# Attention stage with projections: explicit step lists over two images per loop body, and an fp32 product for the last key block

## The chip, the cores and the metric

The kernel runs on one core of a Trainium2 chip. The metric is the device time of one execution in microseconds. A core has five engines with their own instruction queues, each strictly in order: PE (TensorE, matrix products into PSUM), DVE (VectorE), ACT (ScalarE), POOL (GpSimd) and SP (SyncE, which here only issues DMAs). They meet through semaphores: an instruction adds to one when it ends, and another engine's queue waits until a count is reached.

## What is computed

The reference is a chain of six blocks on 32 images of 32 x 32 tokens with 64 channels. The change lies in one of them, attention with projections:

```python
q = jnp.einsum('bnf,of->bno', x, Wq) + bq
k = jnp.einsum('bnf,of->bno', x, Wk) + bk
v = jnp.einsum('bnf,of->bno', x, Wv) + bv
scores = jnp.einsum('bnf,bmf->bnm', q, k) / TEMP      # 1024 x 1024 an image
alpha = jax.nn.softmax(scores, axis=-1)
out = jnp.einsum('bnm,bmf->bnf', alpha, v)
...
t = t + _L3_attn_ref(_ln_t(t), ...)                   # _ln_t: normalise over 64 channels
```

## The kernel before

After a setup the kernel runs five stages, one after the other with a barrier between: the two convolution-like blocks, attention without projections (`stage_attend`, here the second stage), the expert pooling, attention with projections (`stage_attend_qkv`, the fourth stage, 1806 to 2575 us), and the routed experts. All tokens stay in one SBUF tensor, `tokens`.

**Numbers as pairs.** fp32 accuracy is kept with fp16 matmuls by splitting a number into a high and a low fp16 part. Weighing probabilities with values takes three products per key block: high x high, high x low, low x high (L1921, L1923, L1925).

**An image in the fourth stage.** It has 8 query tiles of 128 tokens (NT = 8). Ahead of the tiles come the normalisation (helpers L68 to L138: sum and centring on DVE, square on ACT, sum of squares on DVE, inverse root and scaling on POOL, the high part on ACT, the low part on POOL, eight transposes on PE, a copy on DVE) and five projections through one PSUM bank `ps_w`, each PE, then ACT (high part), then DVE (low part, L1739, L1742, L1745): two halves of q, two halves of k, one v. Then for each tile g:
- range: two matmuls into `ps_a` (L1889), which exists once; DVE takes the negated row maximum (L1767), and SP copies it as a row into `qm` with a small DMA (L1720). Four semaphores `max_rowed` tell when a row has landed.
- score: sixteen matmuls of 128 columns into one of two buffers `ps_s` (L1905, L1907).
- ACT takes the exponential into `pr` (fp32, a ring of RING = 4) at L1823, and its fp16 high part `prh` at L1827; POOL subtracts for the low part `prl` (L1850).
- weigh: 24 matmuls of 65 columns into one of two places of `ps_o` (L1921 to L1925); the 65th column sums the probabilities.
- for every two tiles, DVE takes the reciprocal (L1774) and adds the divided result to `tokens` (L1777, two steps of 64 columns).

**What sets the order.** Each engine's queue is written by `stream` (L1049): for each tile m of an image, `near` (projections of the next image, step m), `step` (range of tile m + 3, score of tile m, weighing of tile m - 3, as far as the engine has a part in it) and `far` (normalisation of the image after that, step m). All engines use the same frame; one image after the next, two images in one loop body. Waits of note: the exponential of tile g waits until POOL's low part of tile g - 4 is done and the high part until tile g - 4 is weighed (L1822, L1826); weighing an even tile waits until the two before it have been added (L1914).

```python
at = tile_at(i, h, m + LEAD)          # PE, step: range of a later tile
at = tile_at(i, h, m) if m >= 0 else None   # score of this one
at = tile_at(i, h, m - LAG)           # weighing of an earlier one
```

Of the kernel before, what the change touches and what calls it, by code (L numbers as in the profile page):

```python
# [6 lines left out]
ALU = mybir.AluOpType  # L7
# [5 lines left out]
P = 128  # L13
# [1639 lines left out]
def stage_attend_qkv(net, d):  # L1653
# [4 lines left out]
    RING, LAG, LEAD = 4, 3, 3  # L1658
    with ExitStack() as ctx:
# [23 lines left out]
        tv = net.t[:].rearrange("p (i h) g c -> p i h g c", h=2)  # L1683
# [7 lines left out]
        def count(at, lag=0):  # L1691

            i, h, m = at
            return NT * (2 * i + h) + m - lag + 1

        def pair_count(at, lag=0):

            i, h, m = at
            return (NT // 2) * (2 * i + h) + (m - lag) // 2 + 1

        def row_count(at, lag=0):

            i, h, m = at
            return 16 * ((NT // RING) * (2 * i + h) + (m - lag) // RING + 1)

        def past(at, lag):

            return tile_at(at[0], at[1], at[2] - lag) is not None

        with nc.Block() as block:  # L1710
            @block.sync
            def _(sp):

                def copy_and_turn(n, h):
                    for k in range(2):
                        sp.wait_ge(proj_high, piece_count(n, PROJ, k))
                        sp.dma_start(qm[h][0:C, half_of(k)], qx[h][0:C, half_of(k)]).then_inc(copied, 16)
                    for g in range(NT):
                        sp.wait_ge(maxed, piece_count(n, NT, g))
                        sp.dma_start(qm[h][C:C + 1, P * g:P * g + P], nmax[:, g:g + 1]).then_inc(max_rowed[g % RING], 16)  # L1720

                sp.wait_ge(set_up, 1)
                with sp.Fori(0, PAIRS) as i:
                    for h in range(2):
                        copy_and_turn(2 * i + h, h)
                sp.wait_ge(copied, 32 * B)
                for r in range(RING):
                    sp.wait_ge(max_rowed[r], 16 * (NT // RING) * B)

            @block.vector  # L1730
            def _(dve):
                def near(i, h, m):
                    n, k = 2 * i + h, m - 1
                    if not 0 <= k < PROJ:
                        return
# [13 lines left out]
                def far(i, h, m):  # L1749
                    n1, w = base + 2 * i + h + 1, wk[h]  # L1750
                    if m == 0:
                        norm_sum(nc, ln, n1, tv[:, i, h], w)
                    if m == 1:
                        norm_centre(nc, ln, n1, tv[:, i, h], w)
                    if m == 2:
                        norm_sumsq(nc, ln, n1, w)
                    if m == 7:
                        take_turned(nc, ln, n1, w, ps_w[:].bitcast(F16))

                def step(i, h, m):  # L1760
                    at = tile_at(i, h, m + LEAD)
                    if at:
                        g = at[2]
                        dve.wait_ge(ranged, count(at))
                        if past(at, NT):
                            dve.wait_ge(max_rowed[g % RING], row_count(at, NT))
                        nc.vector.tensor_reduce(nmax[:, g:g + 1], ps_a[:], AX.X, ALU.max,  # L1767
                                                negate=True).then_inc(maxed, 1)
                    at = tile_at(i, h, m - LAG)
                    if at and at[2] % 2:  # L1770

                        ia, ha, g = at
                        dve.wait_ge(weighed, count(at))
                        nc.vector.reciprocal(rinv[:], outs[:, :, C]).then_inc(inverted, 1)  # L1774
                        dve.wait_ge(inverted, pair_count(at))
                        for k in range(2):
                            ins = nc.vector.scalar_tensor_tensor(tv[:, ia, ha, g - 1 + k], outs[:, k, 0:C],  # L1777
                                                                 rinv[:, k:k + 1], tv[:, ia, ha, g - 1 + k],
                                                                 ALU.mult, ALU.add)
                        ins.then_inc(added, 1)  # L1780

                for h in range(2):
                    set_ones(nc, wk[h])
                    nc.vector.memset(vh[h][:, :, C:C + 1], 1.0)
                    nc.vector.memset(vl[h][:, :, C:C + 1], 0.0)
# [6 lines left out]
                stream(dve, step, near, far, LAG, near_first=True, lead=LEAD)  # L1792
# [3 lines left out]
            def _(act):  # L1796
                def near(i, h, k):
                    if k >= PROJ:
                        return
# [547 lines left out]
```

## Time and profile before

| | |
|---|---|
| median of 3 runs | 2982.1 us (2976.99 to 2982.51) |
| the profiled execution | 2982.43 us, span 2980.6 us |
| PE | busy 2303.2 us, 77% of the span |
| DVE | 2260.9 us, 76% |
| ACT | 2107.7 us, 71% |
| POOL | 1694.9 us, 57% |
| mean granted TensorE clock | 0.921 |
| fourth stage, steady part | about 1866 to 2550 us, clock 1.00 |

The shares are means over stages with different limits. The change touches the fourth stage alone, so it is read in windows of that stage. A busy PE includes the time in which matmuls overlap in the pipeline; for what PE can take, the distance from one start to the next is read. A row of the timeline gives start, length, engine, line and operation, and in brackets the idle time before with what ended it.

### The profile page before, as it was taken

The numbers are of one execution on the slowest core, as the hardware profiler recorded it, in microseconds if no ns is written. First come the engines' busy times: TensorE is split into PE (matmuls) and PEld (weight loads), VectorE is DVE, ScalarE is ACT, GpSimd is POOL, SyncE is SP. The second block draws the span as 40 slices with busy tenths as digits, with TensorE's granted clock in tenths as the row PEclk, the third lists the DMA queues.
The fourth block names the chain that finished last, engine by engine and source line by source line (L and its number), as shares of the span: only waits on it lengthen the run. The fifth ranks groups of instructions, "written<-read, shape, count | busy, mean of one in ns | idle before, by whom it ended". The sixth has DMA issues, their size and how long they took to land. (4 is left out here: it accounts for less than half of the span.)

```text
span 2980.6 us, 85198 instructions
## 1 busy us (share of the span) xinstructions
PE 2303.2 (77%) x32988; PEld 1694.0 (57%) x32988; DVE 2260.9 (76%) x3654; ACT 2107.7 (71%) x3520; POOL 1694.9 (57%) x1370
## 2 busy tenths in 40 slices
PE   3777777787874999999645485888888888777777
PEld 1555555555552676777434473776777677544454
DVE  4677787777774899898766325888888888688887
ACT  2677777777773899999622112888888888677776
POOL 3577777777765222222266202998999899733331
PEclk9999999999996999999856566999999999799999
DMA  3211111111100000000000200000000000001001
GB/s 72 50 44 37 37 39 42 42 36 30 29 22 1 19 18 18 18 18 18 9 0 0 58 0 4 7 5 5 7 5 5 5 7 6 4 22 24 21 21 25
DMA packets 144660, 62.06 MB, mean 21 GB/s; under 512 B 118677, under 2 KB 127799, under 8 KB 144567
## 3 DMA queue, kind: packets, MB, share of 16 engines
q1 hardware_dynamic: 139565, 58.00, 9.1%
q10 hardware_dynamic: 4393, 2.77, 0.4%
q8 instruction: 64, 1.05, 0.1%
q14 instruction: 30, 0.24, 0.0%
q0 software_dynamic: 608, 0.01, 0.0%
HBM read 14.50 MB, written 8.39 MB: 8 GB/s over the span
## 5 line engine op out<-in xcount | busy, mean ns | idle before, releaser
L1850 POOL TENSOR_TENSOR a_prl<-a_pr,a_prh 128x1024 f16<-128x1024 f32 x256 | 544.3, 2139 | 38.1 <-ACT a_prh L1827 36.3
L1767 DVE TENSOR_REDUCE a_nmax<-a_ps_a 128x1 f16<-128x1024 f32 x256 | 312.1, 1219 | 29.3 <-PE a_ps_a L1889 27.3
L1198 DVE TENSOR_TENSOR a_exl<-a_ex,a_exh 128x1024 f16<-128x1024 f32 x224 | 275.6, 1260 | 29.6 <-ACT a_exh L1238 28.5
L1827 ACT ACTIVATE a_prh<-a_pr 128x1024 f16<-128x1024 f32 x256 | 270.6, 1057 | 8.2
L1823 ACT ACTIVATE a_pr<-a_ps_s 128x1024 f32<-128x1024 f32 x256 | 259.4, 1013 | 0.0
L1905 PE MATMUL a_ps_s<-a_qx,a_kh 128*128 128x128 f16 x2048 | 257.9, 220 | 0.3 <-DMA a_qm<-a_nmax 0.3
L1907 PE MATMUL a_ps_s<-a_qm,a_kl 128*128 128x128 f16 x2048 | 257.9, 220 | 0.0
L1233 ACT ACTIVATE a_ex<-a_ps_s,a_shift 128x1024 f32<-128x1024 f32 x224 | 242.9, 1099 | 0.5 <-PE a_ps_s L1281 0.5
L2152 ACT ACTIVATE f_mixed_s<-f_ps_e,f_gates 128x64 f32<-128x64 f32 x1024 | 212.8, 425 | 41.8 <-PE f_ps_e L397 37.0
L1921 PE MATMUL a_ps_o<-a_vh,a_prh 128*128 128x65 f16 x2048 | 216.8, 196 | 3.4 <-POOL a_prl L1850 3.4
L1905 PEld LDWEIGHTS a_ps_s<-a_qx,a_kh 128*128 128x128 f16 x2048 | 200.6, 98 | 31.0 <-issue 1.0
L1907 PEld LDWEIGHTS a_ps_s<-a_qm,a_kl 128*128 128x128 f16 x2048 | 201.1, 98 | 29.9 <-issue 0.6
L114 POOL TENSOR_TENSOR a_w_hl<-a_xn,a_w_hl 128x512 f16<-128x512 f32 x32 | 36.0, 1124 | 318.4 <-ACT a_w_hl L106 318.4
L1923 PE MATMUL a_ps_o<-a_vl,a_prh 128*128 128x65 f16 x2048 | 217.0, 193 | 0.0
L1925 PE MATMUL a_ps_o<-a_vh,a_prl 128*128 128x65 f16 x2048 | 216.1, 193 | 0.0
L1280 PE MATMUL a_ps_s<-a_w_xT 128*128 128x512 f16 x512 | 196.5, 384 | 22.1 <-ACT a_ex L1233 13.0
L1889 PE MATMUL a_ps_a<-a_kh,a_qx 128*128 128x512 f16 x512 | 156.0, 387 | 64.5 <-DVE a_nmax L1767 64.4
L1281 PE MATMUL a_ps_s<-a_w_xT,a_xTb 128*128 128x512 f16 x512 | 195.0, 381 | 0.0
L90 POOL TENSOR_TENSOR f_w_var<-f_w_ss,eps 128x8 f32<-128x8 f32 x64 | 12.8, 200 | 320.1 <-DVE f_w_ss L85 320.1
L1921 PEld LDWEIGHTS a_ps_o<-a_vh,a_prh 128*128 128x128 f16 x2048 | 191.8, 97 | 4.0 <-POOL a_prl L1850 2.6
L1925 PEld LDWEIGHTS a_ps_o<-a_vh,a_prl 128*128 128x128 f16 x2048 | 192.1, 97 | 0.0
L1923 PEld LDWEIGHTS a_ps_o<-a_vl,a_prh 128*128 128x128 f16 x2048 | 191.6, 99 | 0.0
(351 smaller groups left out, 8535.7 us busy)
## 6 DMA issues: line engine op xcount, KB each, us to landing
tokens<-in_x_dram SPq DMA_DIRECT2D x32, 256.0 KB, 2.9
bl_qg<-bl_qk_high SPq DMA_DIRECT2D x128, 64.0 KB, 2.0
bl_km<-bl_qk_high SPq DMA_DIRECT2D x256, 32.0 KB, 2.0
a_xTb<-a_w_xT SPq DMA_DIRECT2D x64, 128.0 KB
out_dram<-tokens SPq DMA_DIRECT2D x32, 256.0 KB, 2.6
bl_qg<-bl_qk_low SPq DMA_DIRECT2D x64, 64.0 KB, 2.0
bl_km<-bl_qk_low SPq DMA_DIRECT2D x128, 32.0 KB, 2.0
a_qm<-a_qx SPq DMA_DIRECT2D x64, 64.0 KB, 2.0
```

The costliest lines, as they stand in the source:

```text
L1198: nc.vector.tensor_tensor(exl[:, at[2]], exps(at), exh[:, at[2]], ALU.subtract).then_inc(low, 1)
L1233: nc.scalar.activation(exps(at), ps_s[:, m % 2], ACT.Exp, bias=shift[:]).then_inc(exped, 1)
L1767: nc.vector.tensor_reduce(nmax[:, g:g + 1], ps_a[:], AX.X, ALU.max, negate=True).then_inc(maxed, 1)
L1823: nc.scalar.activation(pr[:, r], ps_s[:, m % 2], ACT.Exp).then_inc(exped, 1)
L1827: nc.scalar.activation(prh[:, r], pr[:, r], ACT.Copy).then_inc(high, 1)
L1850: nc.gpsimd.tensor_tensor(prl[:, r], pr[:, r], prh[:, r], ALU.subtract).then_inc(low, 1)
L1905: nc.tensor.matmul(out, kh[ha][:, keys], qx[ha][:, queries], start=True, stop=False, skip_group_check=True)
L1907: last = nc.tensor.matmul(out, kl[ha][:, keys], qm[ha][:, queries], start=False, stop=True, skip_group_check=True)
L1921: nc.tensor.matmul(out, high_j, vh[ha][:, j], start=(j == 0), stop=False, skip_group_check=True)
L1923: nc.tensor.matmul(out, high_j, vl[ha][:, j], start=False, stop=False, skip_group_check=True)
L1925: last = nc.tensor.matmul(out, low_j, vh[ha][:, j], start=False, stop=(j == NT - 1), skip_group_check=True)
L2152: ins = nc.scalar.activation(mixed_s[:, h, e, g // 2], ps_e[:, g % BANKS, C * e:C * e + C], ACT.Identity, scale=gates[q][h][:, g, e:e + 1])
```

## The change

`stream` is left for this stage. Each engine gets a written list of steps for one body (one image), and `run_pairs` (L440) lays two bodies into the loop. AHEAD says which image a step belongs to: norm two images ahead, proj, copy, range_next and row_next one ahead, weigh_last and final_last one behind, the others the body's own. The order within a body differs from engine to engine and is no longer one frame by tiles. Among the differences: the exponential now waits for both the low part and the weighing of tile g - 4, and other steps may stand between it and the high part; DVE runs the norm steps 0 and 1 in front of the range step of tile 3; SP issues rows, then the copies, then the rows of the next image; ACT waits before a projection's high part until the image before last is through with the buffer.

```python
def iteration(i, k):                  # run_pairs, L445
    for stream, step in steps:
        n = i + ahead[stream]
        if not isinstance(i, int) or 0 <= n < B:
            streams[stream](n, step, (k + ahead[stream]) % 2)
```

The second part: of 8 key blocks, the last (SPLIT = 7) is weighed as one fp32 matmul from `pr` and a new fp32 tensor `vf`, in front of the others. So the high and the low parts of a tile are 896 columns instead of 1024, DVE gets one more instruction per image (`vf`, 64 columns) and its step for `vl` is 448 columns instead of 512.

```diff
-    RING, LAG, LEAD = 4, 3, 3
+    RING = 4
+    SPLIT = NT - 1
...
+        vf = [sb(f"vf{h}", [P, NT - SPLIT, C + 1], F32) for h in range(2)]
         pr = sb("pr", [P, RING, TOK], F32)
-        prh, prl = (sb(s, [P, RING, TOK], F16) for s in ("prh", "prl"))
+        prh, prl = (sb(s, [P, RING, P * SPLIT], F16) for s in ("prh", "prl"))
...
+        PE_STEPS = [("range", 3), ("proj", 0), ("score", 0), ("score", 1), ("range", 4), ("weigh_last", 5),
+                    ("proj", 1), ("score", 2), ("range", 5), ("weigh_last", 6), ("proj", 2), ("weigh_last", 7),
+                    ("score", 3), ("range", 6), ("weigh", 0), ("score", 4), ("range", 7), ("proj", 3), ("score", 5),
+                    ("weigh", 1), ("range_next", 0), ("proj", 4), ("score", 6), ("range_next", 1), ("weigh", 2),
+                    ("weigh", 3), ("range_next", 2), ("score", 7), ("norm", 5), ("weigh", 4)]
+        DVE_STEPS = [("norm", 0), ("norm", 1), ("range", 3), ("proj", 0), ("norm", 2), ("range", 4),
+                     ("final_last", 2), ("proj", 1), ("range", 5), ("final_last", 3), ("range", 6), ("proj", 2),
+                     ("range", 7), ("proj", 3), ("final", 0), ("range_next", 0), ("range_next", 1), ("proj", 4),
+                     ("final", 1), ("range_next", 2), ("norm", 5)]
+        ACT_STEPS = [("proj", 0), ("norm", 1), ("score", 0), ("proj", 1), ("cut", 0), ("score", 1), ("score", 2),
+                     ("proj", 2), ("cut", 1), ("cut", 2), ("score", 3), ("proj", 3), ("cut", 3), ("score", 4),
+                     ("norm", 4), ("cut", 4), ("score", 5), ("proj", 4), ("cut", 5), ("score", 6), ("score", 7),
+                     ("cut", 6), ("cut", 7)]
+        POOL_STEPS = [("norm", 2), ("cut", 0), ("norm", 3), ("cut", 1), ("cut", 2), ("cut", 3), ("norm", 4),
+                      ("cut", 4), ("cut", 5), ("cut", 6), ("cut", 7)]
+        SP_STEPS = [("row", 3), ("row", 4), ("row", 5), ("row", 6), ("row", 7), ("copy", 0), ("copy", 1),
+                    ("row_next", 0), ("row_next", 1), ("row_next", 2)]
+        AHEAD = {"norm": 2, "proj": 1, "copy": 1,
+                 "range_next": 1, "row_next": 1, "range": 0, "row": 0, "score": 0, "cut": 0, "weigh": 0, "final": 0, "weigh_last": -1, "final_last": -1}
+
+        def run(engine, steps, streams):
+
+            run_pairs(engine, steps, AHEAD, {s: streams[s.removesuffix("_next").removesuffix("_last")] for s, _ in steps})
...
+                def copy(n, k, h):
+                    sp.wait_ge(proj_high, piece_count(n, PROJ, k))
+                    sp.dma_start(qm[h][0:C, half_of(k)], qx[h][0:C, half_of(k)]).then_inc(copied, 16)
+
+                def row(n, g, h):
+                    sp.wait_ge(maxed, count(n, g))
+                    sp.dma_start(qm[h][C:C + 1, P * g:P * g + P], nmax[:, g:g + 1]).then_inc(max_rowed[g % RING], 16)
...
-                        ins = nc.vector.scalar_tensor_tensor(vl[h][:, :, 0:C], tiles(ps_w[:]), IWS,
-                                                             vh[h][:, :, 0:C], ALU.mult, ALU.subtract)
+                        nc.vector.tensor_scalar(vf[h][:, :, 0:C], tiles(ps_w[:])[:, SPLIT:NT], IWS, None, ALU.mult)
+                        ins = nc.vector.scalar_tensor_tensor(vl[h][:, 0:SPLIT, 0:C], tiles(ps_w[:])[:, 0:SPLIT], IWS,
+                                                             vh[h][:, 0:SPLIT, 0:C], ALU.mult, ALU.subtract)
...
+                def take_max(n, g, h):
+                    dve.wait_ge(ranged, count(n, g))
+                    if past(n, g, NT):
+                        dve.wait_ge(max_rowed[g % RING], row_count(n, g, NT))
+                    nc.vector.tensor_reduce(nmax[:, g:g + 1], ps_a[:], AX.X, ALU.max, negate=True).then_inc(maxed, 1)
...
+                    if not isinstance(n, int) or n >= 2:
+                        act.wait_ge(scored if k < 4 else weighed, NT * (n - 1))
...
+                def score(n, g, h):
+                    act.wait_ge(scored, count(n, g))
+                    if past(n, g, RING):
+                        act.wait_ge(low, count(n, g, RING))
+                        act.wait_ge(weighed, count(n, g, RING))
+                    nc.scalar.activation(pr[:, g % RING], ps_s[:, g % 2], ACT.Exp).then_inc(exped, 1)
+
+                def cut(n, g, h):
+                    act.wait_ge(exped, count(n, g))
+                    nc.scalar.activation(prh[:, g % RING], pr[:, g % RING, 0:P * SPLIT], ACT.Copy).then_inc(high, 1)
...
+                def cut(n, g, h):
+                    r = g % RING
+                    pool.wait_ge(high, count(n, g))
+                    nc.gpsimd.tensor_tensor(prl[:, r], pr[:, r, 0:P * SPLIT], prh[:, r], ALU.subtract).then_inc(low, 1)
...
+                def weigh(n, g, h):
+                    if g % 2 == 0 and past(n, g, 1):
+                        pe.wait_ge(added, pair_count(n, g // 2, 1))
+                    if g == 0:
+                        pe.wait_ge(proj_low, piece_count(n, PROJ, PROJ - 1))
+                    pe.wait_ge(low, count(n, g))
+                    out = outs[:, g % 2]
+                    for j in range(SPLIT, NT):
+                        nc.tensor.matmul(out, pr[:, g % RING, P * j:P * j + P], vf[h][:, j - SPLIT], start=(j == SPLIT),
+                                         stop=False, skip_group_check=True)
+                    for j in range(SPLIT):
+                        high_j, low_j = (s[:, g % RING, P * j:P * j + P] for s in (prh, prl))
+                        nc.tensor.matmul(out, high_j, vh[h][:, j], start=False, stop=False, skip_group_check=True)
+                        nc.tensor.matmul(out, high_j, vl[h][:, j], start=False, stop=False, skip_group_check=True)
+                        last = nc.tensor.matmul(out, low_j, vh[h][:, j], start=False, stop=(j == SPLIT - 1),
+                                                skip_group_check=True)
+                    last.then_inc(weighed, 1)
```

## Rows read from the trace of the kernel before

**Rows 1.** Windows view: stretch, length, busy us and count by engine, clock, DMA.
```profile
1865.51:2514.41 648.90, 566.92 (x10412) 457.89 (x10408) 549.96 (x821) 563.32 (x652) 589.77 (x340) 1.00 0.05 6
```

**Rows 2.** Source view of L74: count, min/median/max ns, first and last start.
```profile
L74 DVE SCALAR_TENSOR_TENSOR a_w_xc<-a_w_sum,tokens x29: 2364/2392/2505, 1872.1 to 2514.6; 128x512 f32<-128x512 f32 x29
```

**Rows 3.** Waits view, 1860 to 2550 us: us in total, times, longest.
```profile
PE a_ps_a L1889 <- DVE a_nmax L1767: 59.1, 119, 0.7
...
POOL a_w_var L90 <- DVE a_w_ss L85: 39.8, 29, 1.4
```

**Rows 4.** Timeline of DVE in two images: start us, length us, engine, line.
```profile
2150.64 1.23 DVE L1767 TENSOR_REDUCE a_nmax<-a_ps_a 128x1 f16<-128x1024 f32 x1
2151.78 0.16 DVE L1774 RECIPROCAL a_rinv<-a_ps_o 128x2 f32<-128x2 f32 x1
2152.09 0.47 DVE L1777 SCALAR_TENSOR_TENSOR tokens<-a_ps_o,a_rinv,tokens 128x64 f32 x2 [0.15 <-DVE a_rinv L1774]
2152.48 0.68 DVE L85 TENSOR_REDUCE a_w_ss<-a_w_sq 128x8 f32<-128x512 f32 x1
...
2153.67 1.21 DVE L1767 TENSOR_REDUCE a_nmax<-a_ps_a 128x1 f16<-128x1024 f32 x1
...
2164.98 0.69 DVE L138 COPY a_w_xT<-a_ps_w 128x1024 f16<-128x1024 f16 x1 [0.59 <-PE a_ps_w L128]
...
2167.75 0.68 DVE L69 TENSOR_REDUCE a_w_sum<-tokens 128x8 f32 x1
...
2170.44 2.39 DVE L74 SCALAR_TENSOR_TENSOR a_w_xc<-a_w_sum,tokens 128x512 f32<-128x512 f32 x1
```

**Rows 5.** Timeline of POOL beside that L74.
```profile
2170.15 2.13 POOL L1850 TENSOR_TENSOR a_prl<-a_pr,a_prh 128x1024 f16<-128x1024 f32 x1 [0.22 <-ACT a_prh L1827]
```

**Rows 6.** Timeline of ACT: a P part, C, E, C.
```profile
2154.63 0.60 ACT L1804 ACTIVATE a_kh<-a_ps_w 128x512 f16<-128x512 f32 x1 [0.73 <-PE a_ps_w L417]
...
2169.02 1.06 ACT L1827 ACTIVATE a_prh<-a_pr 128x1024 f16<-128x1024 f32 x1
...
2170.47 1.02 ACT L1823 ACTIVATE a_pr<-a_ps_s 128x1024 f32<-128x1024 f32 x1
2171.51 1.06 ACT L1827 ACTIVATE a_prh<-a_pr 128x1024 f16<-128x1024 f32 x1
```

**Rows 7.** Timeline of ACT, second stage: an exponential right behind another.
```profile
1202.46 1.10 ACT L1233 ACTIVATE a_whole<-a_ps_s,a_shift 128x1024 f32<-128x1024 f32 x1
1203.46 1.10 ACT L1233 ACTIVATE a_ex<-a_ps_s,a_shift 128x1024 f32<-128x1024 f32 x1
```

**Rows 8.** Timeline of PE: starts of P, R, S, W, P4 and R.
```profile
2154.22 0.38 PE L417 MATMUL a_ps_w<-a_w_xT,wb 128*128 128x512 f16 x1
2154.94 0.61 PE L1889 MATMUL a_ps_a<-a_kh,a_qx 128*128 128x512 f16 x2 [0.34 <-DVE a_nmax L1767]
2155.38 0.22 PE L1905 MATMUL a_ps_s<-a_qx,a_kh 128*128 128x128 f16 x1
...
2156.27 0.19 PE L1921 MATMUL a_ps_o<-a_vh,a_prh 128*128 128x65 f16 x1
...
2157.01 0.19 PE L409 MATMUL a_ps_w<-wa,a_w_xT 128*128 128x64 f16 x1
...
2157.48 0.60 PE L1889 MATMUL a_ps_a<-a_kh,a_qx 128*128 128x512 f16 x2
```

**Rows 9.** Timeline, first stage: DVE started ahead of POOL.
```profile
113.55 0.69 DVE L74 SCALAR_TENSOR_TENSOR bl_norm_xc<-bl_norm_sum,tokens 128x512 f32<-128x512 f32 x1
...
113.67 1.59 POOL L114 TENSOR_TENSOR bl_gate_hl<-bl_x,bl_gate_hl 128x512 f16<-128x512 f32 x1 [0.79 <-ACT bl_gate_hl L106]
```

**Rows 10.** Timeline of PE, second stage: fp32 matmuls, two records each.
```profile
1207.67 1.67 PE L1292 MATMUL a_ps_o<-a_xn,a_whole 128*128 128x65 f32 x14
...
1210.48 0.33 PE L1292 MATMUL a_ps_o<-a_xn,a_whole 128*128 128x65 f32 x2
1210.65 0.19 PE L1310 MATMUL a_ps_o<-a_w_hl,a_exh 128*128 128x65 f16 x1
```

More of the change, by code:

```diff
@@ L1756, in far @@
                         norm_sumsq(nc, ln, n1, w)
-                    if m == 7:
+                    if step == 5:
                         take_turned(nc, ln, n1, w, ps_w[:].bitcast(F16))
[L1760 to L1780, printed above, removed]
@@ new lines, in take_max, with final @@
+                def take_max(n, g, h):
[3 more added lines that the diff above has]
+                    nc.vector.tensor_reduce(nmax[:, g:g + 1], ps_a[:], AX.X, ALU.max, negate=True).then_inc(maxed, 1)
+                def final(n, p, h):
+                    dve.wait_ge(weighed, count(n, 2 * p + 1))
+                    nc.vector.reciprocal(rinv[:], outs[:, :, C]).then_inc(inverted, 1)
+                    dve.wait_ge(inverted, pair_count(n, p))
+                    for k in range(2):
+                        ins = nc.vector.scalar_tensor_tensor(net.t[:, n, 2 * p + k], outs[:, k, 0:C], rinv[:, k:k + 1],
+                                                             net.t[:, n, 2 * p + k], ALU.mult, ALU.add)
+                    ins.then_inc(added, 1)
@@ L1791, in _ @@
                 ins.then_inc(set_up, 1)
-                stream(dve, step, near, far, LAG, near_first=True, lead=LEAD)
+                run(dve, DVE_STEPS, {"norm": norm, "proj": proj_low_part, "range": take_max, "final": final})
                 dve.wait_ge(added, B * NT // 2)
@@ new lines, in norm, with rank @@
+                def norm(n, step, h):
+                    if not isinstance(n, int) or n >= 1:
+                        pe.wait_ge(proj_low, PROJ * n)
+                    turn(nc, ln, base + n + 1, wk[h], ps_w[:].bitcast(F16), net.ident16[:])
+                def rank(n, g, h):
+                    if g == 0:
+                        pe.wait_ge(proj_low, piece_count(n, PROJ, PROJ - 2))
+                    if past(n, g, 1):
+                        pe.wait_ge(maxed, count(n, g, 1))
+                    for half in range(2):
+                        keys = slice(512 * half, 512 * half + 512)
+                        last = nc.tensor.matmul(ps_a[:, keys], qx[h][:, P * g:P * g + P], kh[h][:, keys], start=True,
+                                                stop=True)
+                    last.then_inc(ranged, 1)
@@ new lines, in score @@
+                def score(n, g, h):
+                    pe.wait_ge(max_rowed[g % RING], row_count(n, g))
+                    if g == 0:
+                        pe.wait_ge(copied, 32 * n + 32)
+                    if past(n, g, 2):
+                        pe.wait_ge(exped, count(n, g, 2))
+                    queries = slice(P * g, P * g + P)
+                    for j in range(NT):
+                        keys, out = slice(P * j, P * j + P), ps_s[:, g % 2, P * j:P * j + P]
+                        nc.tensor.matmul(out, kh[h][:, keys], qx[h][:, queries], start=True, stop=False,
+                                         skip_group_check=True)
+                        last = nc.tensor.matmul(out, kl[h][:, keys], qm[h][:, queries], start=False, stop=True,
+                                                skip_group_check=True)
+                    last.then_inc(scored, 1)
@@ L1929, in _ @@
                 pe.wait_ge(set_up, 1)
-                stream(pe, step, near, far, LAG, lead=LEAD)
+                run(pe, PE_STEPS, {"norm": norm, "proj": project, "range": rank, "score": score, "weigh": weigh})
 ROUTE_STEPS = [("mix0", 0), ("mix0", 1), ("mix0", 2), ("mix0", 3), ("mix0", 4), ("mix0", 5), ("mix0", 6), ("mix0", 7),
```

166 lines of the change are left out of this document (37 added, 129 removed).

## The prediction

> Short names, for one image of 8 query tiles: R is the range pass of a tile (L1889), M its maximum on VectorE (L1767), S its scores (L1905, L1907), E the exponential, C and L the high and low cut (L1827, L1850), W the weighing (L1921 to L1925), F the final step of two tiles (L1774, L1777), P0 to P4 the projections, T the transposes. A prime marks a tile of the image before, an n one of the image after.
>
> **What bounds the kernel now.** I read the windows view of the middle of the stage first. The granted clock is 1.00 there, so nothing below is a clock effect; POOL is busy 91% of the time, ACT 87%, PE 87%, DVE 85% [rows 1]. No engine is full, and four are nearly so. Next the period: the line that centres the normalisation (L74) starts once an image, from 1872.1 to 2514.6 in 29 starts, so an image takes 642.5 / 28 = **22.95 us** [rows 2]. POOL's busy time in that is 589.8 x 22.95 / 648.9 = 20.9 us; two microseconds are idle everywhere. Where they go the waits show: PE stands 59 us before R until the maximum of the tile before is taken, and POOL 40 us until VectorE's sum of squares has come [rows 3]. PE and DVE pass one buffer (ps_a) and one pair of outputs (ps_o) back and forth in a fixed order by tiles. The DVE timeline shows the worst link: L74 lasts 2.39 us where its fastest instances, in other stages, take 0.69 [rows 4, 9]. Beside it stands a POOL instruction L1850 that started 0.29 us earlier at 2170.15 and ended at 2172.28; L74 ended at 2172.83, 0.55 us later [rows 4, 5]. All 29 instances are 2.36 to 2.51 us long [rows 2]. So a DVE instruction with two SBUF inputs stands still while POOL has one, and this kernel pays it every image. The other order exists too: where L74 starts 0.12 us before a POOL subtraction, L74 takes 0.69 us and POOL 1.59 [rows 9].
>
> **Costs of the change, per image.**
> POOL: L1850 shrinks from 1024 to 896 columns, 2.135 x 7/8 = 1.87 us, eight times: minus 2.1 us. POOL comes down to 18.8 us and is no longer the fullest.
> ACT: C goes from 1.06 to about 0.95 us (1024 columns take 1.06, 512 take 0.60, so 0.9 ns a column) [rows 6]. In the old order E and C of a tile follow each other, with C waiting for E's end: starts 1.04 us apart [rows 6]. In the new order an E is often followed by something that is ready, and then starts are 1.00 us apart for a 1.10 us instruction [rows 7], an overlap of 0.10. I take 0.92 for an E that takes 1.02. ACT falls from 20 to some 18 us.
> DVE: an added tensor_scalar of 64 columns (vf), not in the trace of before. Starts lie about 0.09 us closer than the durations are long (M is 1.23 us, the next start comes after 1.14). A reciprocal of 2 columns, 0.17 us, so makes 0.08; two steps of 64 columns with a second input move the next start by 0.39, 0.20 each. Between these I take 0.14 for vf, in the middle, since its width is that of the one and its single input that of the other [rows 4]. The step for vl is 64 columns shorter, minus 0.07. So DVE does not change by more than 0.1 us, less what L74's wait becomes.
> SP: R rows, copies and rows of the next image go in one written order. Row issues were spread over the whole image and are so again; each M is issued at least 3 us before its S, and the copies stand behind row 7, 7 us before S0 of the next image. I cost that at nothing; were a row late, S would wait by that much.
> PE: from start to start, S is 0.89 us, W 0.74 (24 matmuls, 31 ns each), R 0.43, P the same two 512-column matmuls (0.44), P4 0.47, and T, half as many matmuls as S, 0.45 [rows 8]. That is 8 x (0.89 + 0.74 + 0.43) + 4 x 0.44 + 0.47 + 0.45 = 19.2 us. Of W, three matmuls go (93 ns) and one fp32 matmul of 128x65 comes. The trace has the same form in the second stage: one of them, two records, stands 0.17 us from its start to the next matmul's; of seven in a row each further one adds (1.67 - 0.33) / 6 = 0.22 [rows 10]. The 0.17 comes behind a 512-column matmul that covers its first weight load (0.11 us, half of 0.22). Behind W's own 31 ns matmuls 0.08 of that load is bare, behind S or T 0.05. So W is 0.82 five times, 0.87 twice and 0.90 once: PE becomes 19.98 us. Bounds: 0.17 everywhere gives 19.8, 0.25 everywhere 20.4.
> The page TensorE: Matmul & The Clock Gate of the Trainium skill (LDWEIGHTS, and Weight-path perf modes) says that fp32 weights get no fast load and a load of 128 columns takes about 107 ns. That would put each fp32 block at 0.21 us wherever it stands, an estimate that puts PE at 19.2 + 8 x 0.12 = 20.1 us and the forecast 4 us later; the rows of seven in a row agree with it (0.22), the single one does not (0.17).
>
> **Placing the new body.** PE is now the fullest engine, so I write its steps in order and ask at each whether what it waits for has come, with 0.03 us from PE to its consumer and 0.06 from M to R [rows 4, 6, 8]. The one gives, for instance, a P that starts at 2154.22 and lasts 0.38, and its consumer at 2154.63; the other an M that ends at 2154.88 and R at 2154.94. With R3 at 0: P0 0.43, S0 0.87, S1 1.76, R4 2.65, W5' 3.1, P1 4.0, S2 4.4, R5 5.3, W6', P2, W7' 7.0, S3, R6 8.8, W0, S4, R7 11.0, P3 11.4, S5, W1 12.7, Rn0, P4 14.0, S6, Rn1, W2, W3, Rn2, S7, T, W4. Two places do not fit.
> First, Rn1. F0 waits for W1, then comes Mn0: from W1's start 1.03 + 0.03 + F 0.70 + M 1.22 + 0.06 = 3.04 us, while PE gets there in 0.87 + 0.43 + 0.47 + 0.89 = 2.66. A stall of **0.38**.
> Second, R4. It needs M3, which stands on DVE behind norm steps 0 and 1, and step 1 is L74. From Rn1's start DVE does: R's time 0.63, Mn1 1.14, vf 0.14, vl 0.54 (0.61 less 0.07), F1 0.70, Mn2 1.14, the copy of T 0.60, the sum 0.68 and 0.03 of handing over, and issues L74 at **5.60**. From the same start PE, ACT and POOL do: Rn1 0.43, W2 0.82, W3 0.90, Rn2 0.43, S7 1.08, E7 0.92, C6 0.95, hand over 0.08, and POOL starts L6 at **5.61**. The two are even. A margin of that size is decided by the unknowns: vf (0.05 less, 0.06 more on DVE), the fp32 block (0.1 less, 0.1 more on the other side), and what the end of the loop body costs DVE, which falls exactly between the copy of T and the sum every second image and which I have at nothing. DVE's side has nine links that can only be late, the other side is mostly PE, which runs without waits there. So I take POOL first.
> With POOL first, L74 ends at 5.61 + 1.87 + 0.55 = 8.03, M3 (0.03 and 1.22) at 9.28, R4 starts at 9.34. R3 starts at 4.79 and R4 could at 7.44: a stall of **1.90**. Nothing in the chains ahead of Rn1 changes by it, so it repeats every image.
> Period: 19.98 + 0.38 + 1.90 = 22.3 us, against 22.95: 0.68 x 32 = 22 us less. The lead-in and the end keep the same serial steps (one normalisation, five projections; three tiles weighed at the end), and I cost their difference at nothing, plus or minus 4 us. From the profiled execution's 2982.4 us, which is the median 2982.1 within 0.3: **2960.5 us**. Bounds: 22.0 (all fp32 blocks at their cheapest) to 22.9 (0.25 each, and one more gap missed by 0.3), 2951 to 2981.
> The page SBUF — State Buffer of the Trainium skill (Who interferes with whom) has it that whoever issues first keeps the shared port pair and the other fully blocks; the row shows the held L74 ending 0.55, not 0.69, after POOL, so a full block would add 0.14 us an image, 4 us in all.
>
> **Rivals.**
> VectorE wins the race. If L74 is issued before L6, it takes 0.69, M3 ends at 5.60 + 0.69 + 1.25 = 7.54, R4 starts at 7.60 instead of 7.44. The period is 19.98 + 0.38 + 0.16 = 20.52: 2.43 x 32 = 78 us less, **2905**. Bounds 20.3 to 21.1, 2897 to 2923. For it: an even margin, and that any delay of W2, W3 or S7 that I have missed helps it. Against it: all 29 instances of before lost, and DVE has the longer queue of instructions in front. A mixture, one image held and the next not, lies between the two, near 2935.
> The fp32 block does not pipeline between f16 matmuls. Its two records last 0.33 us to their end [rows 10] and the matmul in front 0.19 [rows 8]; if the array drains before and after, the block costs 0.52 instead of about 0.19, 8 x 0.33 = 2.6 us an image on the fullest engine: 22.3 + 2.6 = 24.9, 2.0 x 32 = 62 us more, **3045**, slower. It decides from 0.09 us more per block (22.3 + 8 x 0.09 = 23.0). The 0.17 us row speaks against it, though it is one transition and in another neighbourhood.
> The change doesn't do what it says: handing the work out in another order ends in other waits of the same sum, since PE and DVE still pass one ps_a and one ps_o. Every M must fall into its gap; with two more misses of 0.3 us the period is 22.9 and the time **2981**.
>
> **How the numbers follow.** POOL first 0.46, VectorE first or a mixture 0.34, the same sum 0.10, fp32 block slow 0.10. Predicted is the first. What a measurement of this kernel can tell from no change is about 0.2%, 6 us. Faster by more: 0.34 + 0.44 = 0.78; within: 0.11; slower: 0.11. The range reaches down to the second case's bound and up to just above the fourth: 2895 to 2988; the likeliest case's own is 2951 to 2981.
>
> **What would show it.** L74 in the stage: 2.3 to 2.4 us (POOL first) or 0.69. PE's wait before R on the maximum: some 70 us over 30 images if POOL wins, under 20 if not. W 0.82 to 0.90 us from start to start. POOL's L1850 at 1.87 us. L74's starts 22.3 us apart. I am wrong if PE is not the engine that the stage waits on, if the fp32 block costs more than 0.3 us, or if an image's exponentials wait for a weighing that PE does later than written above.

## The result, and the profile after

The changed kernel takes **2914.8 us** in the median (2908.8 to 2915.7), the kernel before 2982.1; the ratio is 0.977, 95% interval 0.975 to 0.979. Run again beside the later experiments it took 2915.7. The forecast was 2960.5 with a likeliest range of 2951 to 2981; 2914.8 lies outside that one, inside the wide range (2895 to 2988) and close to the first rival, VectorE wins the race, at 2905. The gain of 67 us is three times the 22 that were forecast.

The profiled execution took 2915.67 us, its span 2913.9. The windows view of the middle of the stage stands against [rows 1]: length, then busy time and count of PE, PE's loads, DVE, ACT and POOL, the clock, DMA.

```profile
1865.51:2450.00 584.49, 574.85 (x10035) 486.09 (x10032) 494.56 (x837) 497.92 (x642) 537.55 (x335) 1.00 0.06 7
```

PE is now busy 98% of the time (87% before), POOL 92%, ACT 85%, DVE 85%, at the same clock. The source view of L74 answers to [rows 2]:

```profile
L74 DVE SCALAR_TENSOR_TENSOR a_w_xc<-a_w_sum,tokens x29: 691/691/692, 1856.4 to 2443.5; 128x512 f32<-128x512 f32 x29
```

No instance is held any more: 0.69 us each, where the 29 of before took 2.36 to 2.51. An image takes (2443.5 - 1856.4) / 28 = **20.97 us**, against 22.95. Now the waits view for 1860 to 2480 us, against [rows 3]:

```profile
POOL a_prl L1854 <- ACT a_prh L1836: 49.4, 61, 1.5
...
PEld a_ps_o L1912 <- issue: 17.1, 42, 0.7
...
PEld a_ps_o L1912 <- DVE tokens L1789: 8.7, 15, 0.6
...
PE a_ps_a L1885 <- DVE a_nmax L1781: 5.7, 28, 0.2
```

PE's 59 us before the range pass are 5.7. (This row counts only the time in which no matmul is recorded as running; how long a stall is, is read from start to start further down.) POOL no longer waits for VectorE's sum of squares at all; it waits for ACT, 49 us, so it has time to spare. How near the outcome was shows in the timelines of one image: DVE from the maximum of the next image's tile 1 on,

```profile
2207.83 1.23 DVE L1781 TENSOR_REDUCE a_nmax<-a_ps_a 128x1 f16<-128x1024 f32 x1 [0.70 <-PE a_ps_a L1885]
2208.97 0.21 DVE L1761 TENSOR_SCALAR a_vf<-a_ps_w 128x64 f32<-128x64 f32 x1
2209.11 0.61 DVE L1762 SCALAR_TENSOR_TENSOR a_vl<-a_ps_w,a_vh 128x448 f16<-128x448 f32 x1
...
2210.33 1.22 DVE L1781 TENSOR_REDUCE a_nmax<-a_ps_a 128x1 f16<-128x1024 f32 x1
2211.46 0.68 DVE L138 COPY a_w_xT<-a_ps_w 128x1024 f16<-128x1024 f16 x1
2212.06 0.68 DVE L69 TENSOR_REDUCE a_w_sum<-tokens 128x8 f32 x1
2212.77 0.69 DVE L74 SCALAR_TENSOR_TENSOR a_w_xc<-a_w_sum,tokens 128x512 f32<-128x512 f32 x1
2213.38 1.22 DVE L1781 TENSOR_REDUCE a_nmax<-a_ps_a 128x1 f16<-128x1024 f32 x1
2214.63 0.69 DVE L1755 SCALAR_TENSOR_TENSOR a_qx<-a_ps_w,a_qx 64x512 f16<-64x512 f32 x1
2215.35 0.69 DVE L85 TENSOR_REDUCE a_w_ss<-a_w_sq 128x8 f32<-128x512 f32 x1
2216.07 1.23 DVE L1781 TENSOR_REDUCE a_nmax<-a_ps_a 128x1 f16<-128x1024 f32 x1
```

and POOL with its low cuts of tiles 6 and 7:

```profile
2212.81 4.25 POOL L1854 TENSOR_TENSOR a_prl<-a_pr,a_prh 128x896 f16<-128x896 f32 x2 [1.17 <-ACT a_prh L1836]
```

What leads up to POOL's start is, on PE, the range pass Rn1 and the scores of tile 7, and on ACT the exponential of tile 7 and the high cuts of tiles 6 and 7:

```profile
2207.19 0.60 PE L1885 MATMUL a_ps_a<-a_kh,a_qx 128*128 128x512 f16 x2 [0.20 <-DVE a_nmax L1781]
...
2209.78 0.22 PE L1898 MATMUL a_ps_s<-a_qx,a_kh 128*128 128x128 f16 x1
```

```profile
2210.87 1.02 ACT L1832 ACTIVATE a_pr<-a_ps_s 128x1024 f32<-128x1024 f32 x1 [0.63 <-PE a_ps_s L1900]
2211.79 1.78 ACT L1836 ACTIVATE a_prh<-a_pr 128x896 f16<-128x896 f32 x2
```

L74 starts at 2212.77, POOL at 2212.81. DVE is first by **0.04 us**, and again in the next images (2233.82 and 2233.86, 2254.70 and 2254.74, 2275.76 and 2275.79); from the sixth start of L74 to the last it is 0.03 or 0.04 every time. Now it is POOL's first cut that stands still: the two take 4.25 us instead of 3.73.

### The profile page after: what moved, and what is told of

Its sections match the earlier page's. It is cut to its first block and busy times, and to the rows that moved or that the text cites. A ratio compares the mean times of both kernels' runs of the same rounds, so it can differ in the third digit from the quotient of the medians.

```text
span 2913.9 us, 84659 instructions
## 1 busy us (share of the span) xinstructions
PE 2318.3 (80%) x32732; PEld 1731.1 (59%) x32732; DVE 2210.4 (76%) x3688; ACT 2045.3 (70%) x3520; POOL 1645.1 (56%) x1370
## 3 DMA queue, kind: packets, MB, share of 16 engines
q8 instruction: 63, 1.03, 0.1%
## 5 line engine op out<-in xcount | busy, mean ns | idle before, releaser
L1854 POOL TENSOR_TENSOR a_prl<-a_pr,a_prh 128x896 f16<-128x896 f32 x256 | 494.6, 1948 | 54.5 <-ACT a_prh L1836 54.5
L1832 ACT ACTIVATE a_pr<-a_ps_s 128x1024 f32<-128x1024 f32 x256 | 261.9, 1024 | 32.5 <-PE a_ps_s L1900 20.3
L1836 ACT ACTIVATE a_prh<-a_pr 128x896 f16<-128x896 f32 x256 | 235.9, 948 | 0.2
L1917 PE MATMUL a_ps_o<-a_vl,a_prh 128*128 128x65 f16 x1792 | 192.3, 192 | 0.0
L1916 PE MATMUL a_ps_o<-a_vh,a_prh 128*128 128x65 f16 x1792 | 192.0, 195 | 0.0
L1918 PE MATMUL a_ps_o<-a_vh,a_prl 128*128 128x65 f16 x1792 | 191.1, 193 | 0.0
L1310 PE MATMUL a_ps_o<-a_w_hl,a_exh 128*128 128x65 f16 x1792 | 185.7, 194 | 1.2 <-DVE a_exl L1198 1.2
L1311 PE MATMUL a_ps_o<-a_w_hl,a_exh 128*128 128x64 f16 x1792 | 185.8, 193 | 0.0
L1313 PE MATMUL a_ps_o<-a_w_hl,a_exl 128*128 128x65 f16 x1792 | 184.8, 193 | 0.0
L658 DVE TENSOR_TENSOR bl_gll<-bl_gel,bl_glh 128x512 f16<-128x512 f32 x128 | 101.8, 797 | 105.6 <-ACT bl_glh L761 103.9
```

The costliest lines, as they stand in the source:

```text
L1832: nc.scalar.activation(pr[:, g % RING], ps_s[:, g % 2], ACT.Exp).then_inc(exped, 1)
L1836: nc.scalar.activation(prh[:, g % RING], pr[:, g % RING, 0:P * SPLIT], ACT.Copy).then_inc(high, 1)
L1854: nc.gpsimd.tensor_tensor(prl[:, r], pr[:, r, 0:P * SPLIT], prh[:, r], ALU.subtract).then_inc(low, 1)
L1917: nc.tensor.matmul(out, high_j, vl[h][:, j], start=False, stop=False, skip_group_check=True)
```

## The experiments

Rn1, in what follows, is the range pass of the next image's tile 1, the point from which both chains are counted; R4, W6' and the other short names are those of the prediction. The theory: what lay between the forecast and the result is which of L74 and POOL's cut of tile 6 is issued first. Its rival: there is no such threshold, the gain is the written order's, and a little time on DVE costs no more than itself. A second pair of theories is about what bounds the new stage, PE or POOL, and a third about which part of the change carries the gain.

**1. A memset ahead of the sum.** One instruction of 128 columns is added.

```diff
+        pad = sb("pad", [P, 128], F32)
                     if step == 0:
+                        nc.vector.memset(pad[:], 0.0)
                         norm_sum(nc, ln, n1, net.t[:, n], w)
```

> The changed kernel with one memset of 128 fp32 columns put in front of the normalisation's sum on VectorE, some 0.15 us. Port race: the centring step is then issued about 0.1 us after POOL's low cut of tile 6 instead of 0.04 us before it, is held until that cut ends plus 0.55 us, the maximum of tile 3 ends 1.9 us later, and an image takes 20.97 + 1.9 = 22.9 us; 2915 + 61 = 2976 us. Rival, no race, the gain is that of the written order and the 0.15 us cost at most themselves: 2915 to 2920 us.

Measured: 2959.3 us, ratio to the kernel before 0.993 (0.991 to 0.994). Its DVE timeline, and POOL's beside it:

```profile
2210.54 0.68 DVE L138 COPY a_w_xT<-a_ps_w 128x1024 f16<-128x1024 f16 x1
2211.19 0.17 DVE L1770 MEMSET a_pad<- 128x128 f32 x1
2211.27 0.63 DVE L69 TENSOR_REDUCE a_w_sum<-tokens 128x8 f32 x1
2211.93 2.38 DVE L74 SCALAR_TENSOR_TENSOR a_w_xc<-a_w_sum,tokens 128x512 f32<-128x512 f32 x1
2214.24 1.21 DVE L1783 TENSOR_REDUCE a_nmax<-a_ps_a 128x1 f16<-128x1024 f32 x1
```

```profile
2211.88 4.18 POOL L1856 TENSOR_TENSOR a_prl<-a_pr,a_prh 128x896 f16<-128x896 f32 x2 [1.15 <-ACT a_prh L1838]
```

From the range pass (Rn1 at 2206.27) to L74 it is 5.66 us here and 5.58 in the changed kernel, 0.08 more. L74 now comes 0.05 us after POOL and takes 2.38 us, from its sixth start on in every image; an image takes 22.70 us. A delay of 0.08 us costs 1.73 us an image and 45 us in all. The time was expected at 2976 and is 17 less: the first five images were not held, and the period grew by 1.73, not 1.9. From the start of S1 to that of R4 PE takes 2.69 us instead of 0.91, 1.78 more: the memset's 0.08, half of the 0.15 that it was given, and the 1.69 that L74 is longer. The other 0.05 comes back at R6 and W0, which are longer in one of two images in the changed kernel and in none here; the waits at R5 and W6' stay as they were.

**2. The same with 512 columns.**

```diff
+        pad = sb("pad", [P, 512], F32)
```

> The same memset with 512 columns, some 0.55 us. Port race: a held centring step ends when POOL's cut ends plus 0.55 us wherever it was issued, so this is as long as with 128 columns, 2976 us within 5. Rival, the delay costs itself: 0.55 x 32 = 18 us more than the changed kernel, 2933 us.

Measured: 2968.6 us, ratio 0.996 (0.994 to 0.997). DVE and POOL:

```profile
2206.38 0.48 DVE L1770 MEMSET a_pad<- 128x512 f32 x1
2206.79 0.62 DVE L69 TENSOR_REDUCE a_w_sum<-tokens 128x8 f32 x1
2207.45 1.98 DVE L74 SCALAR_TENSOR_TENSOR a_w_xc<-a_w_sum,tokens 128x512 f32<-128x512 f32 x1
```

```profile
2206.99 4.18 POOL L1856 TENSOR_TENSOR a_prl<-a_pr,a_prh 128x896 f16<-128x896 f32 x2 [1.17 <-ACT a_prh L1838]
```

L74 is issued 0.46 us after POOL instead of 0.05, lasts 0.40 less and ends at the same place. The period is 22.70 us again. The 9 us between the two kernels' medians are not in the steady part. The profiled executions, 20.8 us apart (2979.0 and 2958.2), show where such a difference lies: this stage is 4.7 us longer, since L74 is held two images earlier, and it starts 13.9 us later (1813.3 against 1799.4), behind stages in which the two kernels do not differ. Such scatter ahead of the stage is in every comparison of medians here; its start lies between 1798.6 and 1813.3 us in the thirteen traces. A memset with four times the columns on the chain costs nothing more per image: the threshold theory stands, the rival is out.

**3. The control, the memset behind L74.**

```diff
                         norm_centre(nc, ln, n1, net.t[:, n], w)
+                        nc.vector.memset(pad[:], 0.0)
```

> The control to the run with a memset of 128 columns: the same memset behind the centring step, in front of the maximum of tile 3. The centring step is issued as early as in the changed kernel and wins; what stands behind it comes 0.08 us later, on a chain with no room at R5 and W6'. Port race: 28 x 0.08 = 2 us more than the changed kernel, 2913 to 2919 us. Rival, any lateness of that size on VectorE costs the 45 us: 2959 us.

Measured: 2913.5 us, ratio 0.978 (0.976 to 0.980). All 32 instances of L74 take 0.69 us and the period is 21.00, 0.03 more than the changed kernel's. The same instruction a place further on costs nothing that the medians show.

**4. The new order without the fp32 block.** SPLIT is 8, and `vf` and its matmuls go.

```diff
-    SPLIT = NT - 1
+    SPLIT = NT
```

> The new order with three fp16 products for all eight key blocks, no fp32 block. VectorE issues the centring step at 5.51 us after the range pass of the next image's tile 1, POOL starts its cut at 5.50: even again. If VectorE is first: PE 19.2 us plus 0.85 of missed gaps is under POOL's 20.9, so POOL bounds at about 21.2 us an image, 2925 us. If POOL is first: 22.0 to 22.3 us, 2952 to 2962 us. A theory by which the fp32 block carries the gain has it near 2980.

Measured: 2923.2 us, ratio 0.980 (0.978 to 0.982). The windows view of 1875 to 2425 us, then DVE's L74 and POOL beside it:

```profile
1875.00:2425.00 550.00, 530.11 (x9559) 424.12 (x9556) 470.38 (x754) 485.65 (x598) 547.96 (x313) 1.00 0.06 7
```

```profile
2196.19 1.15 DVE L74 SCALAR_TENSOR_TENSOR a_w_xc<-a_w_sum,tokens 128x512 f32<-128x512 f32 x1
```

```profile
2192.55 8.88 POOL L1851 TENSOR_TENSOR a_prl<-a_pr,a_prh 128x1024 f16<-128x1024 f32 x4
```

POOL is busy 548.0 of 550 us; it is the bound, 21.17 us an image as expected. The race, expected to be even again, isn't one here: POOL goes through four cuts without a pause, L74 waits 0.46 us for the one in hand and gets in ahead of the next. The kernel before takes 2979.8 beside these runs, so the order alone, which here also frees L74, brings 57 us of the 65 down to 2914.8.

**5. The fp32 block in the old order.** The kernel before with SPLIT = 7, `vf`, and the weighing of the diff; the exponential waits for the weighing of tile g - 4 too, since the fp32 product reads its buffer.

```diff
+    SPLIT = NT - 1
+                        for j in range(SPLIT, NT):
+                            nc.tensor.matmul(out, pr[:, g % RING, P * j:P * j + P], vf[ha][:, j - SPLIT], start=(j == SPLIT),
+                                             stop=False, skip_group_check=True)
-                        for j in range(NT):
+                        for j in range(SPLIT):
```

> The kernel before, old order by tiles, with the last key block as one fp32 matmul and high and low parts of 896 columns. The centring step stays beside a POOL cut and is held in each image, 0.25 us less long; PE gets 0.8 us more. As PE and VectorE alternate there, 22.9 to 23.2 us an image: 2981 to 2990 us. A theory by which POOL bounds the kernel before: its 2.1 us less an image come through, down to 2930.

Measured: 2986.1 us, ratio 1.003 (1.001 to 1.004). The windows view and two waits of 1870 to 2450 us:

```profile
1875.00:2425.00 550.00, 501.90 (x8588) 411.08 (x8589) 455.26 (x712) 453.09 (x548) 449.80 (x286) 1.00 0.05 6
```

```profile
PEld a_ps_a L1894 <- DVE a_nmax L1770: 80.8, 100, 1.1
...
POOL a_w_var L90 <- DVE a_w_ss L85: 32.0, 25, 1.3
```

POOL falls to 82% busy and nothing is gained by it: what POOL did in the kernel before was not its bound. L74 takes 2.01 to 2.05 us in each image, 0.36 less than before. PE's weighings take 0.87 us instead of 0.74, so it gets 1.0 us an image more, not 0.8. The period is 23.12 us, 0.17 more; that the shorter hold and waits that close take back the rest is my reading, no run parts them. Alone the fp32 block costs a little.

**6. Two key blocks in fp32.**

```diff
-    SPLIT = NT - 1
+    SPLIT = NT - 2
```

> The changed kernel with two of eight key blocks in fp32. A second fp32 matmul right behind the first costs 0.21 us instead of three times 0.031, so PE takes 8 x 0.12 = 1 us more an image, POOL 2.1 and ACT 0.9 us less. If PE bounds the new stage: 21.9 us an image, 2942 us. If POOL or ACT bounds it: faster than 2915. The centring step wins its race by 0.17 us.

Measured: 2939.0 us, ratio 0.984 (0.982 to 0.987), 21.68 us an image. The windows view, 1875 to 2425 us:

```profile
1875.00:2425.00 550.00, 543.89 (x8932) 468.40 (x8930) 452.11 (x763) 433.86 (x585) 440.26 (x305) 1.00 0.06 7
```

POOL is down to 80%, ACT to 79%, PE stays at 99%, and the kernel is 24 us slower. So neither POOL nor ACT bounds the new stage. PE does, together with what it still waits for VectorE: its eight weighings are 1.05 us longer in all, and the period grows by 0.71, the waits behind them shrinking by the rest.

The race came out nearer than the 0.17 us expected:

```profile
2164.59 0.69 DVE L74 SCALAR_TENSOR_TENSOR a_w_xc<-a_w_sum,tokens 128x512 f32<-128x512 f32 x1
```

```profile
2164.60 2.19 POOL L1854 TENSOR_TENSOR a_prl<-a_pr,a_prh 128x768 f16<-128x768 f32 x1 [2.30 <-ACT a_prh L1836]
```

DVE is first by 0.01 to 0.02 us, and that is enough in every image. Its chain grew as well: `vf` is twice as wide (0.07 us more), and the final step of tiles 2 and 3, which waits for W3, stands 0.08 us.

**7. Earlier steps on VectorE and POOL.**

```diff
-        DVE_STEPS = [("norm", 0), ("norm", 1), ("range", 3), ("proj", 0), ("norm", 2), ("range", 4),
-                     ("final_last", 2), ("proj", 1), ("range", 5), ...
+        DVE_STEPS = [("norm", 0), ("norm", 1), ("range", 3), ("proj", 0), ("range", 4), ("final_last", 2),
+                     ("norm", 2), ("proj", 1), ("range", 5), ...
-        POOL_STEPS = [("norm", 2), ("cut", 0), ("norm", 3), ...
+        POOL_STEPS = [("cut", 0), ("norm", 2), ("norm", 3), ...
```

> The changed kernel with VectorE's sum of squares moved behind the range step of tile 4 and the final step of the last image's tiles 4 and 5, and POOL's low cut of tile 0 moved in front of the inverse root. If PE waits 0.12 us at R5 and 0.37 at W6' only because VectorE comes late to them, both go and an image takes 20.5 instead of 20.97 us: 28 x 0.47 = 13 us less than the changed kernel, 2902 us. If POOL, busy 92%, is the real bound, nothing is gained (2915) or, as it has less room, a few us are lost.

Measured: **2905.4 us** (2904.3 to 2907.8), ratio 0.974 (0.973 to 0.976), 20.75 us an image. Its PE timeline from R4:

```profile
2208.18 0.61 PE L1885 MATMUL a_ps_a<-a_kh,a_qx 128*128 128x512 f16 x2
...
2210.76 0.59 PE L1885 MATMUL a_ps_a<-a_kh,a_qx 128*128 128x512 f16 x2
2211.19 0.33 PE L1912 MATMUL a_ps_o<-a_vf,a_pr 128*128 128x65 f32 x2
...
2212.24 0.39 PE L416 MATMUL a_ps_w<-a_w_xT,wa 128*128 128x512 f16 x1
```

R5 to W6' is 0.43 us where the changed kernel needs 0.80 (0.80 and 0.70 in turn), and R4 to R5 is 2.58 instead of 2.70. So both stalls were VectorE's lateness. But the period falls by 0.22 only, half of the 0.43 that these two give. W6' to P2 is 1.05 where the changed kernel has 0.92, since P1's low part now comes behind the sum of squares, and another 0.12 us comes up at S5, W1 and S6. Ten us less than the changed kernel in the medians (2905.4 against 2914.8 and 2915.7); the period says 28 x 0.22 = 6. Its median is the lowest of this study, but see the next run.

**8. W1 ahead of S5.**

```diff
-                    ("score", 3), ("range", 6), ("weigh", 0), ("score", 4), ("range", 7), ("proj", 3), ("score", 5),
-                    ("weigh", 1), ("range_next", 0), ...
+                    ("score", 3), ("range", 6), ("weigh", 0), ("score", 4), ("range", 7), ("proj", 3), ("weigh", 1),
+                    ("score", 5), ("range_next", 0), ...
```

> The changed kernel with W1 in front of S5 on PE. The final step and the maximum behind it then come 0.9 us earlier, the stall of 0.37 us at Rn1 shrinks to 0.1, if POOL's cut of tile 1 is there by then, and an image takes 20.7 us: 7 us less than the changed kernel, 2907 us. The race between the centring step and POOL starts after Rn1 and keeps its 0.04 us. If the low cut of tile 1 comes late, no gain, 2915.

Measured: 2911.1 us, ratio 0.976 (0.974 to 0.978). S6, in front of Rn1, takes 1.05 us from start to start instead of 1.26, where 0.89 is its own. The period is (2441.3 - 1859.9) / 28 = 20.76, as in run 7. In the medians, 4 us are inside the scatter of the changed kernel; but the stage itself, from the first memset of `qm` to the next stage's exponential, is 715.9 us long here, 716.0 in run 7 and 721.7 and 721.3 in the two traces of the changed kernel. Both runs gain the same 6 us in the stage, and what parts their medians lies outside it.

**9. The list of run 8 for PE (W1 ahead of S5), and the sum of squares behind R4's maximum only.**

```diff
-        DVE_STEPS = [... ("proj", 0), ("norm", 2), ("range", 4),
+        DVE_STEPS = [... ("proj", 0), ("range", 4), ("norm", 2),
```

> W1 in front of S5, and VectorE's sum of squares behind the range step of tile 4 but still in front of the final step. VectorE then reaches the final step 0.15 us earlier, so 0.12 + 0.15 of the stalls at R5 and W6' go beside the 0.27 at Rn1: 28 x 0.5 = 14 us less than the changed kernel, 2901 us; the POOL inverse root waits 0.2 us more, which its idle time covers. If POOL is the bound: 2915 or more.

Measured: 2911.8 us, ratio 0.976 (0.974 to 0.978); not 2901. The period is 20.81 us. R4 to R5 lost its wait, but R5 to W6' went from 0.70 and 0.80 in turn to 0.87 and 0.96: the final step there still stands behind a maximum and a sum, and the wait only changed its place.

**10. Run 7 and run 8 together.** W1 ahead of S5, and the earlier steps of VectorE and POOL.

```diff
-                    ("score", 3), ... ("score", 5), ("weigh", 1), ("range_next", 0), ...
+                    ("score", 3), ... ("weigh", 1), ("score", 5), ("range_next", 0), ...
-        DVE_STEPS = [... ("proj", 0), ("norm", 2), ("range", 4), ("final_last", 2),
+        DVE_STEPS = [... ("proj", 0), ("range", 4), ("final_last", 2), ("norm", 2),
-        POOL_STEPS = [("norm", 2), ("cut", 0), ("norm", 3), ...
+        POOL_STEPS = [("cut", 0), ("norm", 2), ("norm", 3), ...
```

> W1 in front of S5 together with VectorE's and POOL's exchanged steps (low cut of tile 0 before the inverse root, sum of squares after the final step). Singly they gave 10 and 4 us. If they are independent: 2901 us. But POOL's low cut of tile 1 now comes 1.1 us later, at about 12.7 us after R3, where PE wants it at 11.9, so I expect a stall of 0.5 to 0.8 us at W1 that eats the gain: 2905 to 2915 us.

Measured: 2926.4 us, ratio 0.983 (0.981 to 0.985), slower than either. PE in front of W1, and POOL there:

```profile
2214.32 0.43 PE L1912 MATMUL a_ps_o<-a_vf,a_pr 128*128 128x65 f32 x2 [0.82 <-POOL a_prl L1854]
```

```profile
2211.38 1.04 POOL L98 TENSOR_TENSOR a_w_xn<-a_w_xc,a_w_rstd 128x512 f32<-128x512 f32 x1
2212.38 3.73 POOL L1854 TENSOR_TENSOR a_prl<-a_pr,a_prh 128x896 f16<-128x896 f32 x2
```

P3 starts at 2212.90 and W1 could at 2213.33; it starts at 2214.32, when POOL's cut of tile 1, the first of the two from 2212.38, is there. The stall of 1.0 us is larger than the 0.5 to 0.8 expected, and the period is 21.47 us.

**11. The changed kernel again**, with no edit.

> The changed kernel, unaltered, beside the others on one chip: 2915 us. With it the ten us of the exchanged steps stand or fall: they were 2905.4 beside 2914.8 from another call.

Measured: 2915.7 us (2908.3 to 2921.5), ratio 0.979 (0.977 to 0.981). The median repeats within 1 us, and run 7's 2905.4 stays ten below it; six of the ten are in this stage, as said under run 7.

## Why the prediction was wrong

**The step that failed is the choice between two even ends.** The two chains from Rn1 were put at 5.60 us (DVE) and 5.61 us (POOL). With Rn1 at 2207.19 they measure 2212.77 - 2207.19 = 5.58 and 2212.81 - 2207.19 = 5.62. Link by link: vf moves the next start by 0.14, as taken; the copy 0.60; the range pass to S7 2.59 (2.58); E7 0.92, C6 with the handover 1.02 (1.03). I then said that DVE's side had more links that could only be late, took POOL first, and was wrong. With POOL first L74 was to be held and R4 to stall by 1.90 us; L74 is not held, and R4 waits 0.02. The unknowns in both chains came out at a few hundredths. The two images of a loop pass differ in the period (20.9 and 21.05 us in turn) but not in the margin, 0.04 in both; whether the end of the loop body, which I had as a risk on DVE's side, makes that difference is not shown. The sum could not have told the order: a difference of 0.01 us between two chains of 5.6 is no ground for either, and a bet on the other side would have been luck too. What I wrote of the price was right: a hold adds 1.73 us to the period in the run with the memset, and 1.74 by the forecast (1.90 against 0.16). That this run's 2959 us meets the forecast's 2960.5 is partly luck, see below.

**Who stands still.** The two runs with a memset on either side of L74 show it: 0.04 us ahead L74 is not held, 0.05 us behind it is. The page SBUF — State Buffer of the Trainium skill (Who interferes with whom) says that issue order, not the kind of operation, decides who blocks; these runs agree. On the length of the hold the rows go on disagreeing with a full block: L74 issued 0.05 us after a cut of 1.88 us takes 2.38, so it ends 0.55 after POOL's cut and not 0.69.

**The period of either case was too short by 0.4 us.** The rival had 20.52 and measures 20.97, the forecast had 22.3 and the run with the memset 22.70. The stall at Rn1 was found (0.38 forecast, S6 to Rn1 1.26 - 0.89 = 0.37 measured). The rival's 0.16 at R4 is not there (0.02): the maximum starts 0.61 us behind L74, not 0.72. Missed were R5, 0.12, and W6', 0.37 and 0.27 in turn. Between the maximum of tile 3 and the final step DVE needs 2217.21 - 2213.38 = 3.83 us, and counted as I did it is 3.5: I let every DVE step overlap the next by 0.09. But the low part of q starts 1.25 us after the maximum of tile 3 instead of 1.14, and behind it and behind the sum of squares the next start comes 0.72 us after a 0.69 us instruction (2214.63, 2215.35, 2216.07). The low part of k does not do this: in 48 cases of 48 between 1900 and 2400 us it starts 0.09 us before the maximum in front of it ends, the low part of q 0.03 us after. The one writes partitions 0 to 63, the other 64 to 127; that this is the reason was not tried. The prediction's list counts W6' among the places that fit.

The rest is on PE. Once it has started, W6' takes 0.92 us instead of 0.82, and W0 0.89 in every second image: the fp32 matmul costs 0.27 and 0.24 us there. Run 7, where PE no longer waits in front of W6', has it at 0.17 there, so the forecast left out that a wait in front of a weighing makes its fp32 block dearer as well. 0.12 at R5, 0.32 and 0.10 at W6', 0.03 at W0 and 0.05 at P4 and R6, less 0.14 at R4 and 0.02 at Rn1, come to 0.46, the difference of 0.45 within rounding. Run 7 shows that the two stalls can be had back, and that the period then falls by half of them, because others come up.

**The lead-in was not neutral.** I multiplied by 32 images and put lead-in and end at nothing, plus or minus 4. The first three intervals between starts of L74 are 11.4, 25.1 and 23.8 us before, 60.3 in all, and 46.5 after; from the last one to the last reciprocal it is 60.0 before and 63.2 after. So 10.6 us of the stage's 66 come from there: its 28 steady periods give 55.4. For the rival the factor 32 had put nearly as much there by accident, 4 x 2.43 = 9.7 us, so what parts 2914.8 from its 2905 is the period. For the forecast it had put 3, and 19 in the steady part; the run with the memset gives 8.3 and 10.5 (its first two of 28 intervals without a hold). The two errors cancel, and that is the luck in 2959 against 2960.5.

**What held.** PE: W measures 0.81 and 0.82 behind 512 columns except W6' and W0, 0.87 behind S and T, 0.89 behind another W, against 0.82, 0.87 and 0.90. PE is the fullest engine, and work added to it shows in the time (run 6). The fp32 block does pipeline, so the rival at 3045 is out. POOL's cut takes 1.89 us (1.87), ACT's 0.95. SP's new order costs nothing: no wait for a row appears. The rival by which the new order only moves the waits is out as well: PE's wait for the maximum went from 59 to 6 us.

**Where the 66 us are from**, by the stage's length from its first memset of qm to the next stage's exponential (1806.3 to 2594.0 us before, 1804.4 to 2526.1 after): 787.7 before, 790.5 with the fp32 block alone, 769.0 with both parts and L74 held, 721.7 as changed, 728.2 with the order alone. So alone the fp32 block costs 2.8 us, the new order with the hold still in it then brings 21.5, and the race another 47. How long the old kernel would be without the hold was not tried.

## What to carry to other kernels

When four engines are each at 85 to 90%, place the new order step by step against start-to-start distances from the trace, and treat a fit without room as a stall. Chains that end even are not one forecast but two, and the first thing to try is an instruction of a tenth of a microsecond on either side of the suspected point. A vector instruction with two SBUF inputs beside POOL work wants a place where it is surely first or where POOL rests: here 0.04 us in every image carry 45 us, and a small later change can lose them (0.08 us did). Relieving the fullest engine (POOL, by the fp32 block) brings nothing while two others hand one buffer back and forth; it pays once the order has made that engine the bound.

## What the runs showed of the hardware

- The hold between VectorE and POOL has no soft edge. POOL 0.05 us ahead: 2.38 us for a 0.69 us instruction; VectorE 0.04 us ahead, and even 0.01 (run 6): 0.69. POOL pays in both cases: its pair of cuts takes 4.25 us instead of 3.73 with VectorE first, and 4.18 with POOL first, where the second cut is the longer one.
- Who waits gets in at the next boundary of the other's instructions, even if that one has more in its queue: in the kernel with the order alone L74 takes 1.15 us in the midst of four cuts without a pause, and ends 0.55 us behind the cut in hand.
- A held L74 ends at a fixed place: issued 0.46, 0.29 or 0.05 us after POOL (runs 2, before, 1), it ends 0.55 us after POOL's instruction.
- An fp32 matmul of 128x65 among fp16 ones costs 0.17 to 0.27 us from start to start: 0.17 behind a 512-column matmul, 0.22 behind S or T, 0.25 behind another W, 0.27 where PE had waited in front of it.
- Two VectorE instructions with no wait between them overlap by 0.08 to 0.09 us, but not around the low part of q, which works on partitions 64 to 127 where its neighbours start at 0: there the next start comes 0.03 us after the end. The partitions as the reason were not tried.
